# Adding the scalars' bias in the second node pass: from a GpSimd addition to a three-row product on TensorE

## What is computed

```python
sc0 = h0 @ Wsc0                              # scalars, 64 columns
sc1 = jnp.einsum('ncx,cd->ndx', h1, Wsc1)    # vectors
o0 = B0 @ WB0 + sc0                          # B0, B1: from the messages of the node's edges
o1 = jnp.einsum('ncx,cd->ndx', B1, WB1) + sc1
mu = jnp.mean(o0, 0)
var = jnp.mean((o0 - mu) ** 2, 0)
n0 = (o0 - mu) * jax.lax.rsqrt(var + eps) * gamma0 + beta0
nrm1 = jnp.mean(jnp.sum(o1 * o1, -1) / 3.0, 0)
n1 = o1 * (jax.lax.rsqrt(nrm1 + eps) * gamma1)[None, :, None]
x = x + jnp.concatenate([n0, n1.reshape(n, 3 * C)], -1)
```

## Time and profile before

| | us |
|---|---|
| median of three executions | 2392.77 (2392.5 to 2401.5) |
| the profiled execution, its own time | 2393.98 |
| span of its profile | 2391.9 |

### The profile page before, as it was taken

The page is one execution under the profiler, slowest core; times in us unless marked ns, Lnnn a source line. Parts: engine busy times, 40 slices in busy tenths (PEclk is TensorE's granted clock), DMA queues, the critical chain, the costliest instruction groups (busy, mean ns, idle before and its releaser), DMA issues.

```text
span 2391.9 us, 53054 instructions
## 1 busy us (share of the span) xinstructions
PE 1860.9 (78%) x13930; PEld 1471.4 (62%) x13930; DVE 1820.3 (76%) x8033; ACT 1542.4 (64%) x3485; POOL 1181.8 (49%) x1159
## 2 busy tenths in 40 slices
PE   6968999999998978888857777759999677777200
PEld 4645776677776756555646666647777677777200
DVE  6766887888897865555538888959998799999653
ACT  4746777777787754444436666648887799999100
POOL 2125554555554536777747777753331121211575
PEclk9978999999999989999979999979999899999655
DMA  5673444444443434555436666656665688888775
GB/s 174 240 171 98 149 148 138 141 152 149 141 158 132 152 101 68 80 80 81 80 57 116 120 119 121 113 134 195 195 194 187 205 287 289 288 288 280 236 243 173
DMA packets 195484, 387.11 MB, mean 162 GB/s; under 512 B 50096, under 2 KB 88781, under 8 KB 195366
## 3 DMA queue, kind: packets, MB, share of 16 engines
q1 hardware_dynamic: 122678, 310.43, 38.3%
q0 software_dynamic: 59584, 74.91, 17.2%
q10 hardware_dynamic: 13104, 0.61, 0.6%
HBM read 194.86 MB, written 193.49 MB: 162 GB/s over the span
## 4 chain that ended last, share of the span: by engine, by line
PE 33%; issue 20%; DVE 14%; POOL 12%; ACT 11%; DMA 5%; SPq 2%; another core or an unknown queue 2%; DVEq 0%; ACTq 0%; POOLq 0%
PE bank L755 9%; ACT hb L1007 6%; POOL big L483 5%; PE bank L729 5%; POOL x_tab L494 4%; PE bank L775 3%; DVE x1b L1337 2%; PE bank L860 2%; POOL msg_tab L494 2%; PE bank L884 2%; PE bank L718 2%; DVE st L1351 2%; PE bank L873 2%; ACT ht L1143 2%; PE bank L885 2%
## 5 line engine op out<-in xcount | busy, mean ns | idle before, releaser
L755 PE MATMUL bank<-w_sb,ht 128*128 128x256 f32 x1568 | 405.8, 402 | 6.6 <-issue 6.5
L1259 DVE BATCH_NORM_STATS2 st<-big 128x6 f32<-128x256 f32 x686 | 247.2, 416 | 208.1 <-DMA big<-in_x_dram,idx 125.2
L755 PEld LDWEIGHTS bank<-w_sb,ht 128*128 128x128 f32 x1568 | 291.2, 196 | 87.5 <-issue 54.2
L729 PE MATMUL bank<-ident,hb 128*128 128x128 f32 x1568 | 213.9, 279 | 105.0 <-ACT hb L1007 74.8
L483 POOL DMA_INDIRECT big<-x_tab,idx x196 | 192.2, 981 | 183.6 <-ACT h L1007 126.2
L729 PEld LDWEIGHTS bank<-ident,hb 128*128 128x128 f32 x1568 | 176.2, 142 | 141.5 <-issue 100.4
L462 POOL DMA_INDIRECT node_edge<-node_tab,idx x196 | 188.2, 960 | 134.7 <-DVE x1b L1337 85.9
L973 ACT ACTIVATE h2b<-x1b,rs 128x256 f32<-128x256 f32 x392 | 214.4, 597 | 37.1 <-remote 28.6
L538 POOL TENSOR_TENSOR big<-big,bias 128x256 f32<-128x256 f32 x98 | 71.7, 731 | 329.9 <-ACT hb L1007 283.6
L968 ACT ACTIVATE hb<-big,rs 128x256 f32<-128x256 f32 x392 | 211.8, 589 | 12.5 <-DVE rs L1282 11.3
L1007 ACT ACTIVATE hb<-big,rs 128x256 f32<-128x256 f32 x392 | 213.3, 591 | 1.4 <-DVE rs L1282 1.4
(11 more groups left out here) (242 smaller groups left out, 4725.1 us busy)
## 6 DMA issues: line engine op xcount, KB each, us to landing
big<-in_x_dram SPq DMA_DIRECT2D x97, 512.0 KB
x_tab<-x1b SPq DMA_DIRECT2D x97, 512.0 KB
big<-x_tab SPq DMA_DIRECT2D x97, 512.0 KB
out_dram<-x1b SPq DMA_DIRECT2D x97, 512.0 KB, 2.9
msg_tab<-zeros SPq DMA_DIRECT2D x50, 256.0 KB, 2.2
tpw_tab<-tpb SPq DMA_DIRECT2D x49, 256.0 KB, 2.0
tpb<-tpw_tab SPq DMA_DIRECT2D x49, 256.0 KB
big<-msg_tab SPq DMA_DIRECT2D x49, 256.0 KB
```

Of the source, the lines that this page charges most:

```text
L729: last = nc.tensor.transpose(bank[q][:, (2 * j + k) * P:(2 * j + k + 1) * P], hb[:, s.slot(2, 2), 2 * q + j, k * P:(k + 1) * P], ident[:])
L755: last = mm(y, ht[:, q, (2 * j + k) * P:(2 * j + k + 1) * P], w_sb[:, k, :], start=False, stop=(j == 1 and k == 1))
L1259: last = v.bn_stats(st[:, k, j, :], row)
```

## The change

The bias of the scalars leaves x and goes into PSUM. `statistics` copies three rows of `bias` (all partitions hold the same one), splits them into three bf16 rows with `three_parts`, and writes them twice into `bias3`, once for each of the two node rows in a bank; the other 64 columns of each 128 stay zero, as GpSimd cleared them at the start. In the pass, PE opens each half's bank with a product of `ones_bf` and `bias3`: 3 rows, 2 x 128 columns, into the first 128 of each node row's 256. The four products then accumulate (`start=False`) and no longer start anew. GpSimd's loop over the groups and the wait of DVE for it are gone. The tile `bias` stays, and `f_step` uses it as before.

```diff
@@ -274,6 +274,9 @@
+        bias_f = sb("bias_f", [3, 3, C])
+        bias_bf = sb("bias_bf", [3, 3, C], BF16)
+        bias3 = sb("bias3", [3, 2, P], BF16)
@@ -418,7 +421,7 @@
-            for t in (up_w, lin_w, sc_w, wb_w, zeros, addb):
+            for t in (up_w, lin_w, sc_w, wb_w, zeros, addb, bias3):
                 const(g.memset(t[:], 0.0))
@@ -528,18 +531,6 @@
-            def p2_step(s):
-                if s.live(1):
-                    done(pool, p2["relu"], s, 1)
-                    settle(pool)
-                    x1 = xj(big, s.slot(1, XS), D)[:, :, 0:C]
-                    g.tensor_tensor(x1, x1, bias[:].unsqueeze(1).to_broadcast([P, J, C]), ALU.add
-                                    ).then_inc(p2["biased"].sem, 1)
-
-            pool.wait_ge(fs["weights"].sem, 1)
-            run_groups(pool, 1, p2_step)
@@ -910,11 +901,14 @@
                         pe.wait_ge(p2["ht"].sem, s.at(3) * 2 + q + 1)
+                        mm(bank[2 + q][:].rearrange("p (j d) -> p j d", j=2)[:, :, 0:P], ones_bf[:], bias3[:],
+                           start=True, stop=False)
                         for j in range(2):
                             for k in range(2):
                                 y = bank[2 + q][:, j * D + k * P:j * D + (k + 1) * P]
                                 at = slice((2 * j + k) * P, (2 * j + k + 1) * P)
-                                last = mm(y, ht[:, 2 * s.slot(3, 2) + q, at], fin_w[:, k, :], start=True, stop=True)
+                                last = mm(y, ht[:, 2 * s.slot(3, 2) + q, at], fin_w[:, k, :], start=False,
+                                          stop=(j == 1 and k == 1))
@@ -1587,7 +1581,10 @@
-                v.tensor_tensor(bias[:], g_b[:, 1, :], bias[:], ALU.subtract).then_inc(fs["weights"].sem, 1)
+                one(v.tensor_tensor(bias[:], g_b[:, 1, :], bias[:], ALU.subtract))
+                one(v.tensor_copy(bias_f[:, 0, :], bias[0:3, :]))
+                one(three_parts(one, bias_f, bias_bf, bias3[:, 0, 0:C]))
+                v.tensor_copy(bias3[:, 1, 0:C], bias3[:, 0, 0:C]).then_inc(fs["weights"].sem, 1)
@@ -1614,7 +1611,6 @@
                     landed(dve, y_out, s, 5)
-                    done(dve, p2["biased"], s, 3)
                     add_scalars(0)
```

More of the change, by code:

```diff
@@ L362, in build @@
         fs = named("fs", "chain grams grams_end products z sums var root weights")
-        p2 = named("p2", "biased chain_a chain_b stats root norm relu turned ht y out")
+        p2 = named("p2", "chain_a chain_b stats root norm relu turned ht y out")
         y_in, y_out = reused(x_in, G, XS), sems("y_out", 2)
```

## The result

| | us |
|---|---|
| before, median of five executions | 2392.50 (2389.21 to 2401.5) |
| with the change, median of five | 2420.91 (2419.25 to 2434.65) |
| ratio | 1.0126, 95% interval 1.0103 to 1.015 |

The kernel became 28.4 us slower by the medians (their own ratio is 1.0119), 25 to 36 us by the interval; 33 were forecast. The execution that was profiled is the slowest of the five, with a span of 2432.9 us, 41.0 more than that of before. Of these, 11.1 lie ahead of the statistics, in code that the change leaves alone: the bias's own addition starts at 1879.10, against 1867.98 before. On the chips of the experiments the versions with openers come to it between 1841.2 and 1851.2, those without at 1845.6 and 1853.4, so the openers don't bring this about. Stages are therefore compared each from their own start.

What follows compares the result with a forecast made beforehand. Rings of waits in the second node pass, 3.64 us a step, were taken as the bound. Openers +29, statistics +2.7 and the last groups +1 gave 33 us, so 2426 us (+1.4%), range 2405 to 2437.

Steps and rivals of the forecast that it cites:

- What bounds the kernel: Second node pass: two rings of waits, each 3.64 us a step, set the pace; no engine is full.
- the forecast's signs: Second node pass: DVE idle for PE's products some 0.3 us a step, ACT idle ahead of the root for DVE.
- the ring through PE: Two-step loop of waits, transposes over DVE and ACT to later transposes: 7.28 us; PE has 0.18 to spare.
- ring one: DVE with ACT in the second node pass, aggregation to next aggregation over ACT's square root: 3.64 us a step.
- The third ring: ACT and PE alone in the second node pass (relus, transposes, copies, root): 0.07 us a step in hand.
- What goes is worth nothing: GpSimd's addition, 0.73 us a step, and DVE's wait for it: worth 0, at most 0.07 a step.
- Silence pays: Rival: without GpSimd's SBUF traffic DVE is faster and ring one shortens until the third ring ends it, 2389 us; chance 0.03.
- The opener, c = 0.40: Cost of one opener on PE, two a step: 0.40 us, bounds 0.11 and 0.51, from the edge pass's sibling.
- The cheap opener: Rival: an opener costs its columns only, c = 0.11, 2398 us; with one gap left 0.21, 2407; chance 0.16.
- The step, 3.95: With openers PE closes the two-step ring, 7.90 us: 3.95 a step against 3.64, times 93 steps, +29 us.
- Around the pass: Bias split in the statistics +2.7 us, last two groups' products +1 us; GpSimd's clearing and the final edge rows 0.

Runs made afterwards that it cites:

- the openers of zeros: The kernel before, GpSimd's addition kept, with only the openers added (three rows of zeros, 256 columns): 2404.2 us, ratio 1.0127.

## Why the prediction was right

By its own steps:

- **What bounds the kernel.** Right. DVE waits for the products and the root for DVE, as the forecast's signs had it. Four versions of the openers follow the ring through PE: expected 3.61 and so under ring one's 3.64, measured 3.64; 3.76 and 3.75; 3.70 and 3.70; 4.01 and 4.00. The third ring's 0.07 in hand stayed untested, since no version's mean step came under 3.62.
- **What goes is worth nothing.** Right, and shown by itself: a step of 3.64 and a ratio of 0.9998. "Silence pays" falls.
- **The opener, c = 0.40.** Right in size and in its parts: 0.09 late, 0.21 to the products, 0.10 in the first of them. That what costs is three rows against 128, and not the types, was read from the count stage's rows; the opener of 128 rows shows it. The Trainium skill ("TensorEngine Tiling (Array Packing)", Key Properties) says that a change of tiling mode drains TensorE; it has no number, and it doesn't say that a product of three rows counts as another mode. If it does, these runs agree, with 0.3 us for going there and back; that it does was not shown. The cheap opener falls, and the estimate of 0.11 us from the Trainium skill ("TensorE: Matmul & The Clock Gate", Back-to-back issue gap) holds here for an opener of 128 rows alone.
- **The step, 3.95.** The mechanism was right, the term mis-sized: 3.90 was measured. The working took the time from a half's first product to DVE's addition, 1.20, from the end of the pass. In the steady step it is 1.19 with the opener's 0.10 in it, so 1.09. So PE had 0.28 us to spare and not 0.18, and 0.10 less on a ring over two steps is 0.05 less a step: 4.6 us over 93 steps. With it the ring gives 3.90. Why the place matters is shown in part only, under "What was not expected of the hardware".
- **Around the pass.** Statistics: 2.7 forecast, 2.4 measured. The pass beyond its steady steps: 27.9 less 93 x 0.262 leaves 3.5, where 1 was expected. Of this, 1.0 is four more steps, since the 98 starts of the transposes have 97 steps between them and not 93. Another 1.2 comes behind the last transposes, from which it is 6.48 us to the last addition and was 5.27: the 1 that was forecast. And 1.2 lies in the first eight steps, which the forecast passed over. The pass begins at the lower clock, 1.2 GHz, as it did before. With the change the granted clock is 0.50 from 1880 to 1890 and 0.80 from 1890 to 1900, and the eight products take 2.08 at 1890.30 and 1.16 from 1894.22, 12.4 us into the pass. Before, the transposes at 1876.85, 8.6 us into it, were at full speed (eight in 1.04). PE idles longer ahead of the pass now, 7.96 us in place of 5.52, but that is not the reason: with the openers of zeros it idles 5.52 as before and has its first fast products 12.4 us into the pass too. With the openers over the whole bank the transposes 10.7 us into the pass were the first at full speed. Why the clock rose at these times stays open. The columns of the last two rows are those of the earlier trace rows.

```profile
1890.30 2.08 PE L910 MATMUL bank<-fin_w,ht 128*128 128x128 f32 x8
...
1894.22 1.16 PE L910 MATMUL bank<-fin_w,ht 128*128 128x128 f32 x8
...
1880.00:1890.00 10.00, 6.21 (x26) 5.04 (x26) 5.25 (x25) 5.95 (x13) 0.00 (x0) 0.50 0.00 0
1890.00:1900.00 10.00, 10.00 (x62) 8.52 (x61) 7.29 (x31) 6.21 (x13) 0.00 (x0) 0.80 0.48 162
```

The errors went both ways: 29 + 2.7 + 1 = 33 forecast, 24.4 + 2.4 + 3.5 and -0.5 behind the pass, 30 in the profile, 28.4 between the medians. That the whole time came closer than the step's term is in part luck: the step was 4.6 us too dear, and 2.5 us of starts and uncounted steps were left out.

## What to carry to other kernels

Idle time of an engine covers added work only where the work stands in it. PE idled 0.76 us a step, 0.80 was added, and still a step grew by 0.26. The openers stood ahead of products that had 0.28 us to spare on the way to DVE; the other 0.52 us showed, once in two steps. With one opener moved into the idle time the step was the 3.70 that the other one alone gives. So follow the ring step by step and ask how far each engine is from closing it. And price an operation by how much later the next ones come, not by its busy time: a product of three rows between products of 128 rows is listed at 0.28 us and costs 0.40, with 128 rows 0.11.

## What was not expected of the hardware

- A three-row bias product costs less when its idle rows are filled with zeros: 0.11 in place of 0.40 us. The first node pass and the first edge pass of this kernel have such openers of three rows too; they weren't changed here.
- Under a ring over two steps the steps alternate, 3.66 and 4.14, or 3.82 and 4.19 with the opener over the whole bank. A timeline of one step would give a wrong pace.
- DVE's start behind PE's products is not one number. At the end of the pass it came 1.20 us behind the first of eight after 1.69 us of sleep; without GpSimd's addition and the wait for it 1.16, after 1.68. Behind openers of three rows it is 1.26 there for a group's first half and 1.19 for its second, and 1.19 for both in the steady step; without the opener's 0.10 that is 1.16 and 1.09. The length of the sleep doesn't explain it: with openers of 128 rows it is 1.17 after 1.78 us and 1.16 after 0.41. So 0.04 of the 0.11 went with GpSimd's addition and DVE's wait for it; what the other 0.07 are stays open. Without GpSimd's addition, with the change, and with openers of 128 rows (two pairs):

```profile
2205.47 1.95 PE L907 MATMUL bank<-fin_w,ht 128*128 128x128 f32 x16
2206.63 0.29 DVE L1596 TENSOR_TENSOR x1b<-bank,big 128x128 f32<-128x128 f32 x1 [1.68 <-PE bank L907]
...
2260.81 1.16 PE L910 MATMUL bank<-fin_w,ht 128*128 128x128 f32 x8
...
2262.07 0.29 DVE L1603 TENSOR_TENSOR x1b<-bank,big 128x128 f32<-128x128 f32 x1 [2.06 <-PE bank L910]
...
2196.93 1.06 PE L911 MATMUL bank<-fin_w,ht 128*128 128x128 f32 x8
2198.10 0.29 DVE L1604 TENSOR_TENSOR x1b<-bank,big 128x128 f32<-128x128 f32 x1 [1.78 <-PE bank L911]
...
2202.35 1.06 PE L911 MATMUL bank<-fin_w,ht 128*128 128x128 f32 x8
2203.51 0.29 DVE L1604 TENSOR_TENSOR x1b<-bank,big 128x128 f32<-128x128 f32 x1 [0.41 <-PE bank L911]
```
